# A graph and mixture kernel on one core: bias terms as row products, alternating buffers, and both halves of a split operand stacked

## What is computed

```python
# 1. graph attention, 4 heads
q, k, v = x@Wq+bq, x@Wk+bk, x@Wv+bv          # x: [1250, 512], W: [512, 2048]
agg = segment_sum(softmax_by_dst(q[dst].k[src]/sqrt(512)) * v[src], dst)
x_attn = agg + x@Wskip + bskip
h = layernorm(x_attn@Wlin + blin + x_attn[:, :512])
# 2. four low-rank experts, weights w from a gate
hidden = relu(x @ fc1[e].T);  lo = (hidden @ A[e]) @ B[e];  out = sum_e w_e * (lo @ fc2[e].T)
# 3. edge-mean layer: [x, mean of edge_attr (64)] @ W1 + b1 -> relu -> @ W2 + b2
# 4. multi-head self-attention and a mixture of eight experts
```

## Time and profile before

| | us |
|---|---|
| median of 3 runs (2493.26 to 2499.07) | 2495.25 |
| profiled execution, its own time | 2488.83 |
| its span | 2487.1 |
| TensorE busy (share of the span) | 2133.9 (86%) |
| VectorE busy | 1355.4 (54%) |
| ScalarE busy | 721.2 (29%) |
| GpSimd busy | 465.5 (19%) |

### The profile page before, as it was taken

One profiled execution on the slowest core, in us unless ns is written; L12 is line 12 of the kernel. 1 busy time (PEld: TensorE's weight loads), 2 busy tenths in 40 slices (PEclk: granted clock), 3 DMA queues, 4 the chain that ended last, 5 costly groups with the idle time before them and its releaser, 6 DMA issues. The chain is left out here.

```text
span 2487.1 us, 38054 instructions
## 1 busy us (share of the span) xinstructions
PE 2133.9 (86%) x13514; PEld 1865.0 (75%) x13515; DVE 1355.4 (54%) x2964; ACT 721.2 (29%) x1219; POOL 465.5 (19%) x336
## 2 busy tenths in 40 slices
PE   6767797899999999999984599679797999999666
PEld 5656575799899989989973399567676888888666
DVE  5665786444444444444437522531246787788667
ACT  3442101221212221222210211222224655555521
POOL 3550201000000000000002000240031444544354
PEclk8878898999999999999997799879998899999889
DMA  5551001212021211210011300200034111210433
GB/s 201 171 174 63 27 20 37 96 60 57 28 80 60 56 62 50 57 38 15 15 24 47 140 1 0 72 6 0 26 139 131 26 34 26 50 32 27 146 125 102
DMA packets 78877, 156.63 MB, mean 63 GB/s; under 512 B 7147, under 2 KB 22056, under 8 KB 76995
## 3 DMA queue, kind: packets, MB, share of 16 engines
q1 hardware_dynamic: 67692, 130.11, 17.1%
q10 hardware_dynamic: 6123, 13.70, 1.5%
q0 software_dynamic: 4960, 11.49, 1.5%
HBM read 103.92 MB, written 51.36 MB: 62 GB/s over the span
## 5 line engine op out<-in xcount | busy, mean ns | idle before, releaser
L132 PE MATMUL psum<-pt_hi,xn_hi 125*128 125x250 f32 x800 | 225.5, 282 | 1.6 <-DVE pt_lo L1066 1.6
L133 PE MATMUL psum<-pt_lo,xn_hi 125*128 125x250 f32 x800 | 223.8, 280 | 0.0
L134 PE MATMUL psum<-pt_hi,xn_lo 125*128 125x250 f32 x800 | 222.8, 278 | 0.0
L2015 POOL TENSOR_TENSOR mprob<-mprob,mrden 125x1250 f32<-125x1250 f32 x80 | 181.6, 2271 | 210.5 <-DVE mrden L2116 209.6
L1243 POOL TENSOR_TENSOR x_res<-x_res,beta 125x512 f32<-125x512 f32 x10 | 12.5, 1294 | 898.7 <-DMA x_res<-in_x 898.7
L132 PE MATMUL psum<-xt_hi,t_hi 128*125 128x512 f32 (+1 forms) x480 | 169.3, 353 | 2.8 <-DVE mx L1042 1.8
L133 PE MATMUL psum<-xt_lo,t_hi 128*125 128x512 f32 (+1 forms) x480 | 170.2, 355 | 0.0
L134 PE MATMUL psum<-xt_hi,t_lo 128*125 128x512 f32 (+1 forms) x480 | 169.8, 354 | 0.0
L968 ACT ACTIVATE prob<-prob,nb 125x1250 f32<-125x1250 f32 x40 | 53.7, 1342 | 348.9 <-DVE nb L1047 348.9
L2123 DVE TENSOR_REDUCE mmin<-psum 125x1 f32<-125x512 f32 (+1 forms) x240 | 127.3, 584 | 47.6 <-PE psum L2274 47.4
L132 PEld LDWEIGHTS psum<-pt_hi,xn_hi 125*128 125x128 f32 x800 | 151.2, 189 | 1.8 <-DVE pt_lo L1066 1.8
(11 more groups left out here) (474 smaller groups left out, 6004.4 us busy)
## 6 DMA issues: line engine op xcount, KB each, us to landing
slots_in<-slots_blank SPq DMA_DIRECT2D x12, 1282.5 KB, 10.6
cnt<-edge_counts SPq DMA_DIRECT2D x40, 305.2 KB
q_chunk<-q_store SPq DMA_DIRECT2D x40, 250.0 KB
slots_in<-slots_blank SPq DMA_DIRECT2D x3, 1539.0 KB, 17.1
moe_xg<-slots_in SPq DMA_DIRECT2D x17, 256.5 KB
raw_WqT<-in_WqT SPq DMA_DIRECT2D x4, 1024.0 KB, 5.7
raw_WkT<-in_WkT SPq DMA_DIRECT2D x4, 1024.0 KB, 8.7
raw_WvT<-in_WvT SPq DMA_DIRECT2D x4, 1024.0 KB, 6.5
```

What stands on the lines that cost most here:

```text
L132: nc.tensor.matmul(out, lh, rh, start=start, stop=False)
L133: nc.tensor.matmul(out, lh, rl, start=False, stop=False)
L134: return nc.tensor.matmul(out, ll, rh, start=False, stop=stop)
L2015: nc.gpsimd.tensor_tensor(prob[:, n % 4, :], prob[:, n % 4, :], rden[:, n % 4:n % 4 + 1].broadcast_to([P, N]), ALU.mult).then_inc(p_ready, 1)
```

## The change

- `prepare`, bias terms: the four bias vectors are split into hi and lo and laid out as stationary operands: 16 columns for q and k (`bias_t`, `bias_u`, with zeros around, so that each head's result falls on its own row), 4 for LIN (`bias_l`). TensorE multiplies them by hi and lo of the split matrices and sums over all heads in banks 6 and 7. At the end ScalarE copies the rows out; those for q and k are transposed by TensorE, those for LIN are stored in DRAM (`row_store`). The multiplications on GpSimd and VectorE, `columns`, `take_kq` and `take_lin` are gone.
- `prepare`, buffers and order: LIN has two buffers for the loaded matrix and two for its rest, by even and odd head, and is loaded a head earlier. The rests of Q and K overwrite the loaded matrix in head 0 too. The next Q and K are requested after the narrow products (`kq_rows`), no longer at the end of the product before them. `rest` runs on VectorE. All loads of attributes and x are issued by SP, x in two halves. ScalarE's splits, stores and edge parts are interleaved.
- `graph_output`: the skip matrix is the first load; two products with a 0/1 pattern pick the stored rows.
- `expert_lora`: hi and lo of A stand side by side in one operand of 2 x 64 columns, so 8 products instead of 12; weights and B are doubled to 128 rows.
- `edge_mean_gnn`: hi and lo of the edge mean are stacked in 128 rows, with the edge weights loaded twice: 2 products instead of 3.

```diff
-    first_lo = {Q: at("first_q_lo", [128, KT, D], F32R, 182.5), K: at("first_k_lo", [128, KT, D], F32R, 190.5)}
+    lin_raw = [at("raw_Wlin_even", [128, KT, D], F32, 171.25), raw[LIN]]
+    lin_lo = [at("Wlin_even_lo", [128, KT, D], F32R, 171.25), lo[LIN]]
+    bias_t, bias_u = at("bias_t", [128, 272], F32R, 179.25), at("bias_u", [128, 272], F32R, 180.5)
+    bias_l = at("bias_l", [128, HEADS * KT, 4], F32R, 181.625)
...
         @block.sync
             matrix_in(Q, 0), matrix_in(K, 0)
+            for dst, name in ((g.bq[:], "bq"), (g.bk[:], "bk"), (bvs[:, 0, :], "bv"), (bvs[:, 1, :], "bskip")):
+                sp.dma_start(dst, w[name]).then_inc(cols_in, 16)
             sp.dma_start(dst_p[:], w["dst_groups"]).then_inc(s_load, 16)
...
-            matrix_in(V, 0), matrix_in(LIN, 0), matrix_in(SKIP, 0)
+            matrix_in(V, 0), matrix_in(LIN, 0), matrix_in(SKIP, 0), matrix_in(LIN, 1)
             for h in range(1, HEADS):
-                sp.wait_ge(u_done, unit_of(h - 1, 1, 0))
+                sp.wait_ge(kq_rows, h)
                 matrix_in(Q, h), matrix_in(K, h)
+                if h == 1:
+                    attr_load(0)
                 sp.wait_ge(u_done, unit_of(h - 1, 2, 0))
                 matrix_in(V, h)
+                if h == 1:
+                    attr_load(1)
+                if h == 2:
+                    for q in (2, 3):
+                        sp.wait_ge(part_ready[q % 2], 3)
+                        attr_load(q)
                 sp.wait_ge(u_done, unit_of(h, 0, 0))
-                matrix_in(LIN, h), matrix_in(SKIP, h)
+                matrix_in(SKIP, h)
+                if h + 1 < HEADS:
+                    matrix_in(LIN, h + 1)
+                if h == HEADS - 1:
+                    sp.wait_ge(part_ready[0], 6)
+                    x_half(0)
+                    sp.wait_ge(part_ready[1], 6)
+                    x_half(1)
...
         @block.scalar
+            for h, (a, b) in ((1, (0, 1)), (2, (2, 3))):
+                split_hi(LIN, h)
+                store(h, 0, 0)
+                split_hi(SKIP, h)
+                store(h, 0, 1)
+                edge_part(a, 0)
+                store(h, 0, 2)
+                edge_part(b, 0)
+                store(h, 0, 3)
+                edge_part(a, 1)
+                store(h, 1, 0)
+                edge_part(b, 1)
+                store(h, 1, 1)
+                split_hi(Q, h + 1), split_hi(K, h + 1)
+                store(h, 1, 2), store(h, 1, 3)
+                edge_part(a, 2), edge_part(b, 2)
+                split_hi(V, h + 1)
...
         @block.vector
+            for h, (a, b) in ((1, (0, 1)), (2, (2, 3))):
+                split_lo(LIN, h), split_lo(SKIP, h)
+                rest(a, 0), rest(b, 0)
+                rest(a, 1), rest(b, 1)
+                split_lo(Q, h + 1), split_lo(K, h + 1)
+                add_skip(h)
+                split_lo(V, h + 1)
...
         @block.tensor
+            def bias_rows(h, out, cols, i, first, last_of_all):
+                halves = (hi[i], lower(i, h))
+                for k in range(KT):
+                    for j, half in enumerate(halves):
+                        last = nc.tensor.matmul(out, cols(k), half[:, k, :], start=first and k == j == 0,
+                                                stop=last_of_all and k == KT - 1 and j == 1)
+                return last
+
             for h in range(HEADS):
                 product(h, 0, Q, K)
-                columns(h, 6, (0, 1), kq_cols, kq_taken)
+                bias_rows(h, core.bank(6)[0:16, :], lambda k: bias_t[:, 64 * h + 16 * k:64 * h + 16 * k + 16], K, h == 0, False)
+                bias_rows(h, core.bank(6)[0:16, :], lambda k: bias_u[:, 64 * h + 16 * k:64 * h + 16 * k + 16], Q, False,
+                          h == HEADS - 1).then_inc(kq_rows, 1)
                 product(h, 1, V, LIN)
...
-                columns(h, 7, (2, 3), lin_cols, lin_taken)
+                last = bias_rows(h, core.bank(7)[0:4, :], lambda k: bias_l[:, KT * h + k, :], LIN, h == 0, h == HEADS - 1)
...
                 product(h, 2, SKIP, LIN)
...
                 for k in range(KT):
-                    last = three_pass(nc, core.bank(5)[:, 0:CH], [a[:, e, k, :] for a in (a_hi, a_lo)],
-                                      [a[:, k, :] for a in (h_hi[e % 2], h_lo[e % 2])],
-                                      e == k == 0, e == NE - 1 and k == KT - 1)
+                    for i, half in enumerate((h_hi[e % 2], h_lo[e % 2])):
+                        last = nc.tensor.matmul(core.bank(5)[:, 0:CH], a_both[:, e, k, :, :].rearrange("p i r -> p (i r)"),
+                                                half[:, k, :], start=e == k == i == 0,
+                                                stop=e == NE - 1 and k == KT - 1 and i == 1)
...
-                    three_pass(nc, out, [a[:, cols] for a in (e1_hi, e1_lo)],
-                               [a[:, bass.ds(CH * c, CH)] for a in (at_hi, at_lo)], False, True).then_inc(u_done, 1)
+                    for i, half in enumerate((e1_hi, e1_lo)):
+                        last = nc.tensor.matmul(out, half[:, cols], at_both[:, bass.ds(CH * c, CH)], start=False, stop=i == 1)
+                    last.then_inc(u_done, 1)
```

More of the change, by code:

```diff
@@ L379, in _ @@
+            bias_tops()
+            split_hi(V, 0), split_hi(LIN, 0), split_hi(SKIP, 0)
             for m in range(KT):
                 store(0, 0, m)
-            for m in range(KT):
-                store(0, 1, m)
+            store(0, 1, 0), store(0, 1, 1)
             split_hi(Q, 1), split_hi(K, 1)
-            edge_part(0, 0), edge_part(1, 0)
+            store(0, 1, 2), store(0, 1, 3)
             split_hi(V, 1)
-            store(1, 0, 0), store(1, 0, 1)
-            split_hi(LIN, 1)
@@ L410, in _ @@
+            split_hi(LIN, 3)
             store(3, 0, 0), store(3, 0, 1)
-            split_hi(LIN, 3)
+            split_hi(SKIP, 3)
             store(3, 0, 2), store(3, 0, 3)
-            split_hi(SKIP, 3)
+            act.wait_ge(kq_rows, HEADS)
+            nc.scalar.activation(tu_rows[:], core.bank(6)[0:16, :], ACT.Copy).then_inc(tu_out, 1)
             ln.root(nc, act)
@@ L456, in take_kq @@
[L456 to L469 removed]
+                nc.vector.tensor_tensor(lower(i, h)[:], raw_of(i, h)[:], f32(hi[i][:]), ALU.subtract).then_inc(lo_done[i], 1)
@@ new lines, in bias_rests, with rest @@
+            def bias_rests():
+                dve.wait_ge(bias_hi, 1)
+                for dst, src, top in zip(bias_views(1), bias_columns(), bias_views(0)):
+                    last = nc.vector.tensor_tensor(dst, src, f32(top), ALU.subtract)
+                last.then_inc(bias_ready, 1)
+            def rest(q, n):
+                s, use = q % 2, q // 2
+                dve.wait_ge(part_ready[s], 3 * use + n + 1)
+                own = ring[s][:, 0:count[q], :]
+                nc.vector.tensor_tensor(own, own, g.parts[:, quarter[q], n * EDGE_D:(n + 1) * EDGE_D],
+                                        ALU.subtract).then_inc(rest_ready[s], 1)
@@ L1289, in _ @@
         def _(pe):
-            pe.wait_ge(diag_ready, 1)
+            pe.wait_ge(pick_ready, 1)
+            pe.wait_ge(lin_in, 16)
             for i in range(2):
-                for k in range(KT):
-                    last = nc.tensor.matmul(core.bank(6 + i)[0:P, k * 128:(k + 1) * 128], ones[:],
-                                            diag[:, i * KT + k, :], start=True, stop=True)
-                last.then_inc(row_done, 1)
+                nc.tensor.matmul(core.bank(6 + i)[0:P, :], pick[:, i, :], lin_rows[:], start=True, stop=True).then_inc(row_done, 1)
             pe.wait_ge(gs_lo, 1)
```

309 lines of the change are left out of this document (124 added, 185 removed).

## The result

The changed kernel takes 2434.5 us (median of 4 runs, 2430.2 to 2436.3) against 2497.2 us of the kernel before on the same chip (4 runs, 2493.3 to 2502.0): ratio 0.975, 95% interval 0.974 to 0.977. Forecast were 2420 us, range 2398 to 2455. The sign and the range hold; the gain is 62.7 us by the medians, 54.3 us between the two profiled executions (2488.8 and 2434.5). The first stage, the largest part of the forecast, gave half of what was expected.

What follows compares the result with a forecast made beforehand. First-stage waits (61 us) and, in most later stages, TensorE's own time bound the kernel. Terms -41 - 6 - 8.5 - 19 = -74.5 from the profiled 2488.8 gave 2414, with 6.4 to the median 2420 us; range 2398 to 2455.

Steps and rivals of the forecast that it cites:

- first stage: Loop over heads in prepare: fewer TensorE waits, x requested at 139.4, stage end 216 against 256.9, so -41 us.
- Expert stage: expert_lora: 8 low-rank products instead of 12 per chunk and expert; -8.5 us (-6 to -11).
- the forecast's three terms for it: Expert stage: 80 fewer low-rank products -9.4 us, one border per chunk gone -1.0, late hid_lo +1.2.
- the late hid_lo: Expert stage: last low-rank group of each chunk waits for hid_lo, 0.25 us in each of five chunks, +1.2 us.
- Skip products' stage: graph_output: skip matrix loaded first, no longer behind three broadcast rows priced at 6 us; -6 us (-3 to -7.5).
- Edge-mean: Edge-mean stage: unit of 2.14 us becomes 1.64, 40 units; -19 us (-17 to -20.5; only -4 if borders stay).
- rival 4: Edge-mean stage: the 0.19 us at borders comes from something else and stays; +15 us, 2435 us; chance 0.04.
- Narrow products: First stage: 96 products with 16 or 4 stationary columns cost 0.228 us each, plus 3.2 us for 16 borders.
- rivals 1 and 2: First stage: narrow products at f32 price, 0.86 us (2465, chance 0.14); or also at half clock, 1.7 us (2533, chance 0.03).
- SKIP's load in head 2: First stage: load queued behind two attribute loads takes up to 23 us, has 14; stall 0 to 8, taken as 4.
- its own signs: First stage: no TensorE wait over 10 us, about 6 before x transposes; wrong if TensorE waits for ScalarE in heads 1 and 2.
- Rival 3: First stage: nearly full, in-order ScalarE falls behind in heads 1 to 3, x later; gains 15 to 25, 2441 us; chance 0.15.

Runs made afterwards that it cites:

- edge_units: Changed kernel with four kinds of edge-mean unit in turn: 14 or 15 products, the weight products of 128 or 64 rows; 2447.1 us (one run).
- attr_only: Changed kernel with only the edge-attribute quarters loaded as 112 + 13 partitions, ScalarE's order and x load unchanged; 2408.4 us, ratio 0.966.
- pad_pe: Changed kernel with 13 tiny f32 products, read by nobody, added at the head of TensorE's stream; 2424.7 us, ratio 0.972.
- before_dve: Kernel before the change with 50 tiny fills on VectorE inside its first wait; 2493.8 us (one run).

## Why the prediction was right and where it was wrong

**The sign and the stacked products: right.** Expert stage -7.9 for -8.5. Its loop shortened from 30.9 to 29.1 us a chunk, so 9.2 us in five, the sum of the forecast's three terms for it; the late hid_lo costs the 0.25 us a chunk that it gave (0.15 us ahead of the product that waits, 0.10 us behind it). Skip products' stage -8.5 for -6: the products begin 9.4 us after the stage's first transfer instead of 17.0; that is 7.6 us, where I had priced the three rows in front at 6. Edge-mean -23.0 for -19: the unit shortened as forecast (2.14 to 1.62), and the borders were the larger part of it, 0.19 us each as forecast (edge_units); rival 4 is out. What I did not foresee is the clock: in the kernel before, every second chunk ran its first 15 us at 0.89, and its chunks took 29.9 and 31.5 us in turn; after, none of those I looked at does, and they take 26.0 to 26.2. First row before, second after:

```profile
1687.40:1702.40 15.00, 14.95 (x64) 11.99 (x64) 1.38 (x2) 0.00 (x0) 0.00 (x0) 0.89 0.00 0
```

```profile
1653.30:1668.30 15.00, 14.96 (x80) 12.67 (x81) 1.80 (x3) 1.05 (x3) 0.00 (x0) 1.00 0.00 0
```

**Narrow products: right, their borders wrong.** 0.233 us each for 0.228; rivals 1 and 2 are out. The 3.2 us for 16 borders were nothing. I had taken the price of a border in rows (64 against 128) for one in columns (16 against 128). The Trainium skill ("TensorEngine Tiling (Array Packing)", Key Properties) says that a change of tiling mode drains TensorE. The 0.19 us at a border in rows agree with a drain; at a border in columns none shows, and whether a product with 16 or 4 stationary columns changes the mode at all, no run here tells.

**First stage: the step that was wrong.** The time lies in the forecast's own range of 2404 to 2439, but by its own signs the mechanism of this stage was not the one forecast: TensorE had two waits over 10 us (15.7, and 11.8 ahead of the x transposes, for which about 6 was given), and ScalarE was what TensorE waited for in heads 1 and 2, named there as a sign of being wrong. The forecast said that SKIP's load in head 2 takes up to 23 us and stalls TensorE by 0 to 8 us, "I take 4". It took 29.6 us and stalled it by 15.7; head 1, for which I had no stall, lost 5.1 + 1.3. Behind each wait TensorE's products start at half clock, another 2 us a head: head 1 took 46.8 us and head 2 57.1, against 38.3 and 38.6 in attr_only. Head 2 ended at 159.9 instead of 138.9, and x was asked for 20.9 us late. x then needed 27.9 us instead of 24, and from its first use to the end 48.8 instead of 53. Together 20.9 + 3.9 - 4.2 = 20.6 of the 21 us between -41 and -19.9.

I had the cause in hand and drew half of it. The trace of before showed x alone at a third of the engines, and I used it for x only. The attribute quarters have 125 rows too: two of them, 2.7 MB, went at a share of 0.31, and the matrix asked for behind them came 29.6 us after its request; as 112 + 13 rows, 12.1 us. My reading is that the matrix is spread over all 16 engines and ends when the slowest of them has worked off the attributes; the runs fit it, and no view here shows the engines one by one. With the attributes spread, the forecast's other steps come out, some 7 us early: x requested at 132.8 for 139.4, of which 4 are the stall that I had taken, and stage end 209 for 216.

**Rival 3** named the place (ScalarE, heads 1 to 3), the chain and the size (first stage 15 to 25, total 2441; measured 19.9, 2434.5), at a chance of 0.15. Its reason, a ScalarE with too much work, is not what the runs show: with the same order and the same work nothing waits once the loads are on time, and there ScalarE is busy for 25.7 of 38.6 us in head 2, not for the 33 of 39 that I had counted. The total of 2434.5 us is nearer to this rival's 2441 than to my 2420.

**Unchanged code: not considered.** I gave it zero. It cost 10.7 us in graph attention, by the place of its loop in TensorE's stream (pad_pe), and gave 6.1 back behind the edge-mean stage, of which VectorE's pauses are a part (before_dve: 3.2 us) and the rest is open. That the total stayed in my own range is in part luck: 21 us not gained in the first stage and 10.7 us lost here were offset in part by 6.1, 4.0 and 2.5 us that I had not counted, and the 6.4 us added for the distance between the profiled execution and its median did not show: the profiled execution of the changed kernel (2434.5) is its median. The sum of the six terms with their measured sizes, -19.9 + 10.7 - 8.5 - 7.9 - 23.0 - 6.1, is the -54.7 of the two spans.

## What to carry to other kernels

Look at the share of DMA engines beside each load's time before pricing a queue: here loads of 125 partitions held up the matrix behind them, and cutting them (112 + 13 for 125) was worth more (22 to 28 us for the attributes, 8 to 10 for x) than the reordering around them (4 us, or nothing). No other partition count was tried. A wait at an in-order engine names who stands in front, not who is late; follow it to the transfer. A product that starts behind a border or a wait costs time on both sides of its own start: take the distance of starts over a whole unit before pricing it. And a change of program length moves loops in the instruction stream: compare the stages without a changed line too, and book their difference by itself.

## What the runs showed of the hardware

- A pause at a jump back in a loop over heads was 1.5 to 1.9 or 4.1 to 5.2 us long by the place of the loop in TensorE's stream (pad_pe); behind the longer one the first products ran at half clock (0.57 us for 0.38; granted clock 0.85 and 0.87 over the 20 us behind it, 1.00 behind the shorter one). The Trainium skill ("Runtime: NRT & Kernel Launch", Instruction fetch mechanics) says that a taken branch to a page outside the loaded window waits for a transfer; the packets of the instruction queue agree: in five pauses of both lengths the products went on 2.7 to 3.5 us after the second packet began.
- A border between products of 128 and of 64 rows costs 0.19 us in either direction, half ahead of the first product behind it and half behind that product; one between 128 and 16 stationary columns costs nothing that shows (0.23 us from product to product on both sides of it).
- Loads of 125 rows moved 161 GB/s at a share of 0.43 with other traffic; the same bytes as 112 + 13 rows moved 295 GB/s at 0.99. With two loads of 125 rows asked for, 132 GB/s moved at 0.31, and a matrix of 1 MB asked for behind them was read 29.6 us after its request, 12.1 us with the loads in front split.
